# Experts' phase: the high and low parts of the 16 left-over rows as one operand

## The chip, the core and the metric

The kernel runs on one core of a Trainium2 chip. Time is device microseconds of one launch, lower is better. The engines of the core are named as the profile names them: PE is TensorE (with PEld for its weight loads), ACT is ScalarE, DVE is VectorE, POOL is GpSimd, and SP is the engine that here only issues DMAs. A name with a q behind it (PEldq, ACTq) is the sequencer of that engine.

## What is computed

Two layers over 16 sequences of 1024 tokens of width 256. The first layer normalizes, runs a recurrence and a mixture of experts, and multiplies the two; the second does the same with another recurrence and other experts. The change touches only the experts of the first layer:

```python
capacity = max(1, int(Sz * CAP_FACTOR / E) + 1)          # 1024 * 2 / 8 + 1 = 257
scores = softmax(einsum('bsd,ed->bse', x, router_w))
gate_vals, sel_idx = jax.lax.top_k(swapaxes(scores, 1, 2), capacity)
tokens = x[b_idx, sel_idx]                                # per expert 16 x 257 rows of 256
h = gelu(einsum('becd,edh->bech', tokens, w1) + b1, approximate=False)   # hidden width 1024
y = einsum('bech,ehd->becd', h, w2) + b2
out = zeros.at[b_idx, sel_idx].add(y * gate_vals[..., None])
```

Each of the 8 experts takes 257 rows of each of the 16 sequences: 4096 rows in 8 blocks of 512, and 16 rows left over, one of each sequence.

## The kernel before

The phases follow one another: routing, the first recurrence, the experts (`experts_phase`), layer 1. In `experts_phase` every engine has its own program, and semaphores alone order them. Each engine loops over experts 0 to 6 with one body and then runs expert 7 as straight code (`experts`, line 328; the loop itself, with its branch, has line 330).

**Precision.** Products run in float32r. To keep float32 accuracy each operand is split in a high part (a float32r copy, made by ACT) and a low part (the rest, made by DVE), and `product` (line 607) adds three matmuls for one: high x high, low x high, high x low. All of these matmuls have line 611.

**An expert on PE** (`one`, from line 640). Blocks q = 0 to 7 of 512 rows; for each of the 8 chunks m of the hidden width the up product (2 chunks of 128 of the input width, so 6 matmuls of 512 columns) is followed by one eighth of the down products of the block before (`down(e, q - 1, m)`, 12 matmuls of 256 columns). In the middle of a block (m = MID = 3) PE transposes the rows of the next block, or in the last block the 16 left-over rows (`turn_last`). For each m, ACT computes two gelus, one kept in float32 (`hf`) and one in float32r (`hTh`), and DVE subtracts them for the low part.

**The end of an expert.** Block 7's down products have no up products beside them: eight steps s = 0 to 7 (lines from 657). The left-over rows' up products go with the first four: 2 chunks of the hidden width in each step, 12 matmuls of 16 columns, 48 in all, into the bank `ps[2]`. After s = 3 PE transposes the first block of the next expert (`turn(e + 1, 0)`). Once all 48 are done ACT computes sixteen gelus of 128x16 (lines 477 and 478), with the bias b1 as the activation's own bias, and DVE makes the low part from them in one subtraction (line 562). ACT then makes the high part of the next expert's w1 (`split_up`, 434), DVE the low part (494), which lets SP issue the load of the w1 after that (342). The left-over down products (24 matmuls of 256 columns into `ps[4]`, with the 16 rows padded to 128 by zeros from two memsets at the phase's start, line 356) are PE's last work of the expert; DVE adds b2 (571) and multiplies by the gate (573), and POOL scatters the 16 rows (419). ACT's first step in the next turn of the loop is a gelu on one column (456), in front of which it loads its table.

**Waits that the change touches.** `up_ps` counts up products, and one more for all left-over ones; `hi_sb` counts gelus (8 of them for the left-over rows); `h_sb` low parts; `down_ps` halves of a block's down products and the left-over ones; `padded` the memsets. The banks `ps[0]` and `ps[1]` (tiles ps_heads in the profile, with ps[2] and ps[3]) hold transposes.

Of the kernel before, what the change touches and what calls it, by code (L numbers as in the profile page):

```python
# [5 lines left out]
ALU = mybir.AluOpType  # L6
# [251 lines left out]
def experts_phase(nc, ctx, ps, xn_d, acc_d, w1, b1, w2, b2, ident, idxT, gateT, idxL, gateL):  # L258

    with ExitStack() as mem:  # L260
        def sb(name, shape, dt=F32):
            return mem.enter_context(nc.sbuf_tensor(name, shape, dt))
# [23 lines left out]
        xTl = [sb(f"e_xTl{n}", [P, KD, B], F32R) for n in "hl"]  # L286
        hfl = sb("e_hfl", [P, HC, B])
        hTl = [sb(f"e_hTl{n}", [P, HC, P], F32R) for n in "hl"]
# [20 lines left out]
        down_ps = sem("e_down_ps")  # L309
        y_sum = sem("e_y_sum")  # L310
# [6 lines left out]
        HIGHS = QN * HC + HC  # L317
# [3 lines left out]
        MID = HC // 2 - 1  # L321
        W2_PARTS = 4
# [28 lines left out]
        def _(pool):  # L351
# [3 lines left out]
            for part in hTl:  # L355
                nc.gpsimd.memset(part[:].bitcast(F32), 0.0).then_inc(padded, 1)
# [74 lines left out]
        def _(act):  # L431
# [18 lines left out]
            def turn_last(e):  # L450
                act.wait_ge(turned, TURNS * e + QN + 1)
                nc.scalar.copy(xTl[0][:], ps[0][:, 0:KD * B].rearrange("p (k n) -> p k n", k=KD)).then_inc(xh_sb, 1)

            def one(e, last):
# [19 lines left out]
                act.wait_ge(up_ps, UPS * (e + 1))  # L474
                for m in range(HC):
                    z = ps[2][:, m * B:(m + 1) * B]
                    nc.scalar.activation(hfl[:, m, :], z, ACT.Gelu, bias=b1s[:, m:m + 1])
                    nc.scalar.activation(hTl[0][:, m, 0:B], z, ACT.Gelu, bias=b1s[:, m:m + 1]).then_inc(hi_sb, 1)
                if not last:

                    act.wait_ge(hi_sb, HIGHS * (e + 1) + 1)
                    split_up(e + 1)
                    turn(e + 1, 0)

            act.wait_ge(padded, 2)
# [5 lines left out]
        def _(dve):  # L491
# [24 lines left out]
            def turn_last(e):  # L516
                dve.wait_ge(xh_sb, TURNS * (e + 1))
                nc.vector.tensor_tensor(xTl[1][:], ps[0][:, 0:KD * B].rearrange("p (k n) -> p k n", k=KD),
                                        xTl[0][:].bitcast(F32), ALU.subtract).then_inc(xT_sb, 1)
# [23 lines left out]
            def one(e, last):  # L543

                dve.wait_ge(gts_set, 3 * e + 3)
                for q in range(QN):
                    for m in range(HC):
# [14 lines left out]
                nc.vector.tensor_tensor(hTl[1][:, :, 0:B], hfl[:], hTl[0][:, :, 0:B].bitcast(F32), ALU.subtract  # L562
# [8 lines left out]
                nc.vector.tensor_tensor(yl[:], ps[4][0:B, 0:D], b2s[0:B, :], ALU.add).then_inc(y_sum, 1)  # L571
# [13 lines left out]
        def _(pe):  # L585

            def turn(e, q):
                r = q % 2
                pe.wait_ge(x_in[r], 32 * QN * e + 64 * (q // 2) + 64)
                if not (isinstance(e, int) and e == 0 and q == 0):  # L590

                    pe.wait_ge(xT_sb, TURNS * e + q)
                for k in range(KD):
# [45 lines left out]

            def one(e, last):  # L640
# [13 lines left out]
                pe.wait_ge(xT_sb, TURNS * (e + 1))  # L654

                pe.wait_ge(hi_sb, HIGHS * e + HC * QN)
# [15 lines left out]
            pe.wait_ge(padded, 2)  # L672
# [1556 lines left out]
```

## Time and profile before

| | |
|---|---|
| Time, median of 3 runs | 4614.92 us (4613.5 to 4615.97) |
| Span of the profiled execution | 4612.0 us |
| Mean granted TensorE clock | 0.971 |
| Busy, share of the span | PE 91%, DVE 60%, ACT 43%, POOL 37% |
| Experts' phase, on PE | 1895 to 3510 us of the span |
| Slices of PE in that phase | 9 tenths or more in nearly each |

The page gives busy times of one execution. A busy PE is not a PE at its peak, since matmuls are pipelined and overlap: their duration is longer than the distance from one to the next. "issue" is idle time for which the profile shows no releaser. The granted clock is 1.00 for 2.4 GHz and 0.50 for 1.2 GHz.

### The profile page before, as it was taken

Reading aid. Unit: us, or ns where it says so; the run is one execution under the profiler, and the core shown is the slowest. Engines: PE = TensorE matmul, PEld = TensorE weight load, DVE = VectorE, ACT = ScalarE, POOL = GpSimd, SP = SyncE. Lnnn points to the kernel's source line nnn. Section 1 sums busy time; section 2 is a strip of 40 time slices with the busy share of each in tenths; the row PEclk is TensorE's granted clock in tenths of the full one; section 3 lists DMA queues with packets and bytes.
Section 4 is the critical chain, followed back from the end, with each engine's and each line's share of the span. In section 5 each row is a group of like instructions: output and inputs, shape, how many; then the busy total and the mean of one; then the engine's idle time right before and its main releaser. Section 6 shows DMA issues by size and latency. Waiting matters only on the chain. (4 is left out here: it accounts for less than half of the span.)

```text
span 4612.0 us, 79916 instructions
## 1 busy us (share of the span) xinstructions
PE 4189.6 (91%) x28828; PEld 3314.9 (72%) x28828; DVE 2751.5 (60%) x5151; ACT 1976.9 (43%) x3701; POOL 1694.4 (37%) x1338
## 2 busy tenths in 40 slices
PE   6759999999999999799999999999995989999985
PEld 6636555555555556698888989898995878777774
DVE  4447777777767777334343433434433688888886
ACT  2214444444444444444454444445442444444441
POOL 1123333333333333344444444444432233333333
PEclk9999999999999999899999999999997999999998
DMA  6611011011011010223223232323224334444433
GB/s 205 214 44 38 29 38 34 29 38 34 29 38 34 29 38 29 81 42 64 48 56 60 41 66 43 62 47 59 42 40 92 93 98 111 105 95 111 101 61 41
DMA packets 254043, 294.80 MB, mean 64 GB/s; under 512 B 21600, under 2 KB 226656, under 8 KB 251616
## 3 DMA queue, kind: packets, MB, share of 16 engines
q0 software_dynamic: 88064, 117.74, 15.2%
q1 hardware_dynamic: 140000, 138.26, 9.3%
q10 hardware_dynamic: 25600, 33.56, 2.2%
q8 instruction: 260, 4.26, 0.4%
q14 instruction: 119, 0.97, 0.1%
HBM read 155.15 MB, written 134.35 MB: 63 GB/s over the span
## 5 line engine op out<-in xcount | busy, mean ns | idle before, releaser
L523 DVE TENSOR_TENSOR e_hTl<-e_hf,e_hTh 128x512 fp32r<-128x512 f32 x512 | 355.0, 693 | 795.4 <-ACT e_hTh L465 795.4
L1018 POOL TENSOR_TENSOR a_mix<-a_tmp,a_h 128x512 f32<-128x512 f32 x320 | 393.9, 1251 | 808.4 <-DVE a_tmp L1105 651.9
L384 POOL DMA_INDIRECT acc_d<-e_y,e_sids x256 | 402.0, 1570 | 715.6 <-DVE e_y L539 670.8
L464 ACT ACTIVATE e_hf<-ps_heads,e_b 128x512 f32<-128x512 f32 x512 | 355.3, 694 | 697.8 <-PE ps_heads L611 690.6
L611 PE MATMUL ps<-e_w2h,e_hTh 128*128 128x256 f32 x2048 | 580.1, 283 | 0.0
L611 PE MATMUL ps<-e_w2h,e_hTl 128*128 128x256 f32 x2048 | 576.5, 281 | 0.0
L611 PE MATMUL ps<-e_w2l,e_hTh 128*128 128x256 f32 x2048 | 571.3, 279 | 0.0
L611 PE MATMUL ps_heads<-e_xTh,e_w1h 128*128 128x512 f32 x1024 | 419.4, 410 | 26.8 <-issue 22.8
L611 PE MATMUL ps_heads<-e_xTh,e_w1l 128*128 128x512 f32 x1024 | 407.6, 398 | 0.0
L611 PE MATMUL ps_heads<-e_xTl,e_w1h 128*128 128x512 f32 x1024 | 407.2, 398 | 0.4 <-issue 0.3
L611 PEld LDWEIGHTS ps<-e_w2h,e_hTh 128*128 128x128 f32 x2048 | 385.0, 188 | 19.8
L611 PEld LDWEIGHTS ps<-e_w2h,e_hTl 128*128 128x128 f32 x2048 | 385.0, 188 | 17.8
L611 PEld LDWEIGHTS ps<-e_w2l,e_hTh 128*128 128x128 f32 x2048 | 386.7, 189 | 0.0
L1408 PEld LDWEIGHTS ps_heads<-a_R,a_K 32*128 32x128 f32 x7168 | 227.0, 188 | 205.9 <-issue 204.2
L465 ACT ACTIVATE e_hTh<-ps_heads,e_b 128x512 fp32r<-128x512 f32 x512 | 351.3, 686 | 0.0
L1105 DVE SCALAR_TENSOR_TENSOR a_tmp<-ps,a_xb,a_delta 128x512 f32<-128x512 f32 x320 | 239.3, 750 | 174.9 <-PE ps L1317 160.8
L361 POOL DMA_INDIRECT e_x<-xn_d,e_gids x256 | 269.8, 1054 | 190.2 <-PE ps_heads L595 112.4
L1408 PE MATMUL ps_heads<-a_R,a_K 32*128 32x64 f32 x7168 | 256.8, 278 | 62.9 <-DVE a_A L1144 34.2
L1144 DVE COPY_PREDICATED a_A<-a_mask,ps_heads 128x1024 f32<-128x1024 uint32 x160 | 274.4, 1715 | 0.0
L1317 PE MATMUL ps<-a_x,a_xo 128*128 128x512 f32 x512 | 246.6, 604 | 0.7 <-ACT a_R L1231 0.7
L611 PEld LDWEIGHTS ps_heads<-e_xTh,e_w1h 128*128 128x128 f32 x1024 | 195.8, 191 | 66.9 <-issue 28.5
L611 PEld LDWEIGHTS ps_heads<-e_xTl,e_w1h 128*128 128x128 f32 x1024 | 195.3, 191 | 47.4
(294 smaller groups left out, 9458.6 us busy)
## 6 DMA issues: line engine op xcount, KB each, us to landing
r_x<-in_L_attn_hidden_states SPq DMA_DIRECT2D x32, 512.0 KB, 4.6
xn_d<-r_xn ACTq DMA_DIRECT2D x32, 512.0 KB, 3.1
xnT_d<-r_xT ACTq DMA_DIRECT2D x32, 512.0 KB, 3.6
acc_d<-a_zeros POOLq DMA_DIRECT2D x32, 512.0 KB, 3.0
s_d<-a_s SPq DMA_DIRECT2D x32, 512.0 KB, 2.8
e_w<-in_L_ffn_w SPq DMA_DIRECT2D x16, 1024.0 KB, 4.8
f_a<-acc_d SPq DMA_DIRECT2D x32, 512.0 KB, 3.8
f_x<-s_d SPq DMA_DIRECT2D x32, 512.0 KB, 5.2
```

Of the source, the lines that this page charges most:

```text
L361: pool.indirect_dma_start(xg[r][:, t, :], None, xn_d, bass.IndirectOffsetOnAxis(ap=gids[:, GT * q + t:GT * q + t + 1], axis=0)).then_inc(x ...
L384: pool.indirect_dma_start(acc_d, bass.IndirectOffsetOnAxis(ap=sids[:, GT * q + t:GT * q + t + 1], axis=0), ys[r][:, t, :], None, compute_o ...
L464: nc.scalar.activation(hf[m % 2][:], ps[2 + m % 2][:], ACT.Gelu, bias=b1s[:, m:m + 1])
L465: nc.scalar.activation(hT[q % 2][0][:, m, :], ps[2 + m % 2][:], ACT.Gelu, bias=b1s[:, m:m + 1]).then_inc(hi_sb, 1)
L523: nc.vector.tensor_tensor(hT[q % 2][1][:, m, :], hf[m % 2][:], hT[q % 2][0][:, m, :].bitcast(F32), ALU.subtract).then_inc(h_sb, 1)
L611: last = nc.tensor.matmul(out, lhsT, rhs, start=(first and n == 0), stop=(end and n == len(pairs) - 1))
L1018: nc.gpsimd.tensor_tensor(mix[n][:, m, :].rearrange("p (c t) -> p c t", c=GT), tmp[i % 2][:].rearrange("p (c t) -> p c t", c=GT), h[q % 2] ...
L1105: stt(out=tmp[i % 2][:], in0=bank(MIX[i])[:], scalar=xb[:, n, m:m + 1], in1=delta[r][:, m].rearrange("p c t -> p (c t)"), op0=ALU.add, op1 ...
L1144: nc.vector.copy_predicated(a4, m4.unsqueeze(1).to_broadcast([P, NH * GT, nb, half]), pairs_ps(half)).then_inc(A_sb, 1)
L1317: done = nc.tensor.matmul(to, lhsT, rhs, start=(k == 0), stop=(k == len(pairs) - 1))
L1408: done = nc.tensor.matmul(ps_heads[:, hd, c * P:c * P + P // 2].rearrange("p (n t) -> p n t", t=half), K2[r][rows, tok], R2[r][rows, tok]. ...
```

## The change

The high and low parts of the 16 left-over rows lie side by side in one tile and are one operand.

- Up: `xTl` is one tile with 32 columns (16 high, 16 low). Each chunk takes w1's high and low part times these 32 columns: 4 matmuls of 32 columns for 6 of 16, so 32 an expert for 48 (`up_last`). The fourth product, low x low, comes with it. They go to `ps[1]` and are placed in block 7 behind the up and down products of m = 4 to 7, two chunks each time.
- DVE adds the bias to the high columns and then the low columns, two adds of 128x128 into `zl`, and ACT computes two gelus of 128x128 on `zl` for the sixteen. `hi_sb` counts one for them.
- Down: `hTl` is one tile of 128 columns, the high part in columns 0 to 15, the low part in 32 to 47, the rest zeros from one memset. 16 matmuls for 24. The result stands on two groups of partitions; ACT copies the low one (`tl`, 16x256), DVE adds b2 to the high one and then `tl`.
- New waits: DVE waits for `up_ps` before the first add; ACT for `zl_o`, and at the end of the expert for `down_ps`; DVE for `tl_sb`; PE for `zl_o` before it transposes the next expert's first block, which overwrites `ps[1]`. PE no longer waits for the last gelus before the left-over up products.

```diff
@@ ACT, one(e, last)
-                act.wait_ge(up_ps, UPS * (e + 1))
-                for m in range(HC):
-                    z = ps[2][:, m * B:(m + 1) * B]
-                    nc.scalar.activation(hfl[:, m, :], z, ACT.Gelu, bias=b1s[:, m:m + 1])
-                    nc.scalar.activation(hTl[0][:, m, 0:B], z, ACT.Gelu, bias=b1s[:, m:m + 1]).then_inc(hi_sb, 1)
+                act.wait_ge(zl_o, 2 * e + 2)
+                nc.scalar.activation(hfl[:], zl[:], ACT.Gelu)
+                nc.scalar.activation(hTl[:, :, 0:B], zl[:], ACT.Gelu).then_inc(hi_sb, 1)
...
+                act.wait_ge(down_ps, DOWNS * (e + 1))
+                nc.scalar.copy(tl[:], ps[4][LOW_AT:LOW_AT + B, 0:D]).then_inc(tl_sb, 1)
@@ DVE, one(e, last)
+                dve.wait_ge(up_ps, UPS * (e + 1))
+                parts = ps[1][:, 0:HC * 2 * B].rearrange("p (m n) -> p m n", m=HC)
+                nc.vector.tensor_tensor(zl[:], parts[:, :, 0:B], b1s[:].unsqueeze(2).to_broadcast([P, HC, B]), ALU.add
+                                        ).then_inc(zl_o, 1)
+                dve.wait_ge(zl_o, 2 * e + 1)
+                nc.vector.tensor_tensor(zl[:], parts[:, :, B:2 * B], zl[:], ALU.add).then_inc(zl_o, 1)
                 result(e, QN - 2, 1)
...
-                nc.vector.tensor_tensor(yl[:], ps[4][0:B, 0:D], b2s[0:B, :], ALU.add).then_inc(y_sum, 1)
+                nc.vector.tensor_tensor(yl[:], ps[4][0:B, 0:D], b2s[0:B, :], ALU.add).then_inc(yl_o, 1)
+                dve.wait_ge(yl_o, e + 1)
+                dve.wait_ge(tl_sb, e + 1)
+                nc.vector.tensor_tensor(yl[:], yl[:], tl[:], ALU.add).then_inc(y_sum, 1)
@@ PE
+            def up_last(m, last):
+                for k in range(KD):
+                    for n, v in enumerate(w1p):
+                        ups = nc.tensor.matmul(ps[1][:, m * 2 * B:(m + 1) * 2 * B], v[:, k, m * P:(m + 1) * P], xTl[:, k, :],
+                                               start=(k == 0 and n == 0), stop=(k == KD - 1 and n == 1))
+                if last:
+                    ups.then_inc(up_ps, 1)
...
+                        if q == QN - 1 and m > MID:
+                            if m == MID + 1:
+                                pe.wait_ge(xT_sb, TURNS * (e + 1))
+                            for n in (2 * (m - MID) - 2, 2 * (m - MID) - 1):
+                                up_last(n, n == HC - 1)
                 for s in range(HC):
-                    if s <= MID:
-                        for m in (2 * s, 2 * s + 1):
-                            ups = product(ps[2][:, m * B:(m + 1) * B], [([w[:, k, m * P:(m + 1) * P] for w in w1p],
-                                                                         [v[:, k, :] for v in xTl]) for k in range(KD)])
-                        if s == MID:
-                            ups.then_inc(up_ps, 1)
                     down(e, QN - 1, s)
...
-                product(ps[4][:, 0:D], [([v[:, m, :] for v in hTl], [w[:, m, :] for w in w2p]) for m in range(HC)]
-                        ).then_inc(down_ps, 1)
+                for m in range(HC):
+                    for n, v in enumerate(w2p):
+                        done = nc.tensor.matmul(ps[4][:, 0:D], hTl[:, m, :], v[:, m, :], start=(m == 0 and n == 0),
+                                                stop=(m == HC - 1 and n == 1))
+                done.then_inc(down_ps, 1)
```

## Rows read from the trace of the kernel before

**Rows 1.** Groups by line, PE, 1895 to 3515 us: busy, mean ns, idle before

```profile
L611 PE MATMUL ps_heads<-e_xTh,e_w1h 128*128 128x512 f32 x1024 | 419.4, 410 | 26.8 <-issue 22.8 <-DVE e_xTl L512 2.6 <-ACT e_hTh L465 0.5
...
L595 PE MATMUL ps_heads<-ident,e_x 128*128 128x128 f32 x512 | 67.2, 275 | 14.9 <-DMA e_x<-xn_d,e_gids 14.9
```

**Rows 2.** Timeline of PE (start, duration), left-over up products of expert 0

```profile
2077.92 0.17 PE L611 MATMUL ps_heads<-e_xTlh,e_w1h 128*128 128x16 f32 x1
...
2079.38 0.28 PE L611 MATMUL ps<-e_w2h,e_hTl 128*128 128x256 f32 x1
```

**Rows 3.** Timeline of PE: left-over down products, then the next expert

```profile
2095.52 0.28 PE L611 MATMUL ps<-e_w2h,e_hTlh 128*128 128x256 f32 x1
...
2098.24 0.28 PE L611 MATMUL ps<-e_w2l,e_hTlh 128*128 128x256 f32 x1
2101.88 0.79 PE L611 MATMUL ps_heads<-e_xTh,e_w1h 128*128 128x512 f32 x1 [3.36 <-issue]
```

**Rows 4.** Loop lines (330 experts, 895 recurrence, 1615 layer 1): ns min/median/max, first and last start

```profile
L330 ACTq COMPARE_BRANCH  x7: 40/45/50, 2090.7 to 3306.3; - x7
...
L330 PEldq COMPARE_BRANCH  x7: 82/5407/6047, 2096.3 to 3311.9; - x7
...
L895 PEldq COMPARE_BRANCH  x6: 83/4320/4557, 692.4 to 1683.0; - x6
...
L1615 PEldq COMPARE_BRANCH  x2: 83/1826/3570, 4042.8 to 4294.1; - x2
```

**Rows 5.** SP's timeline; DMA queues and issues (size, us to landing) around the branch

```profile
2095.05 0.33 SPq L342 DMA_DIRECT2D e_w<-in_L_ffn_w  x1
...
q1 hardware_dynamic: 288, 1.05, 52.1%
...
q8 instruction: 1, 0.02, 1.0%
...
e_w<-in_L_ffn_w SPq DMA_DIRECT2D x1, 1024.0 KB, 4.6
```

**Rows 6.** Timelines of DVE and ACT at the end of expert 0

```profile
2078.00 0.69 DVE L523 TENSOR_TENSOR e_hTl<-e_hf,e_hTh 128x512 fp32r<-128x512 f32 x1 [2.12 <-ACT e_hTh L465]
...
2090.42 0.29 DVE L562 TENSOR_TENSOR e_hTll<-e_hfl,e_hTlh 128x128 fp32r<-128x128 f32 x1 [10.48 <-ACT e_hTlh L478]
2092.53 2.29 DVE L494 TENSOR_TENSOR e_w1l<-e_w,e_w1h 128x2048 fp32r<-128x2048 f32 x1 [1.82 <-ACT e_b L435]
...
2099.79 0.27 DVE L506 COPY e_b<-e_b2i 128x256 f32<-128x256 f32 x1
...
2093.49 1.28 ACT L456 ACT_TABLE_LOAD   x1
```

**Rows 7.** Timeline of POOL, last expert's left-over scatter

```profile
3513.04 1.30 POOL L419 DMA_INDIRECT acc_d<-e_yl,e_sidl  x1 [0.30 <-issue]
```

**Rows 8.** Timeline of POOL at the start of the experts' phase

```profile
1886.41 0.95 POOL L356 MEMSET e_hTll<- 128x1024 f32 x1
```

**Rows 9.** Groups by line, ACT in the recurrence

```profile
L1240 ACT ACTIVATE a_A<-ident,a_own 128x128 f32<-128x128 f32 x512 | 153.2, 387 | 1.0
```

**Rows 10.** Stretches: length, busy (count) of PE, PEld, DVE, ACT, POOL; granted clock; DMA

```profile
2101.88:2105.10 3.22, 3.22 (x8) 2.54 (x9) 0.00 (x0) 0.26 (x1) 2.61 (x3) 0.50 0.59 65
...
sum 99.87, PE 98.45 PEld 72.70 DVE 51.73 ACT 75.87 POOL 68.15; mean PE 16.41 PEld 12.12 DVE 8.62 ACT 12.64 POOL 11.36
...
3313.94:3328.64 14.70, 14.47 (x64) 10.62 (x63) 10.08 (x20) 12.64 (x22) 10.22 (x10) 1.00 0.41 57
```

**Rows 11.** Two gaps in layer 1 (PE's timeline) and the stretch behind each

```profile
3669.96 1.09 PE L2051 MATMUL ps_heads<-ident,f_xn 128*128 128x128 f32 x8 [2.81 <-ACT f_xn L1958]
...
3787.25 1.17 PE L2051 MATMUL ps_heads<-ident,f_xn 128*128 128x128 f32 x7 [2.15 <-ACT f_xn L1958]
...
3670.00:3673.40 3.40, 3.40 (x30) 3.40 (x31) 3.27 (x6) 2.15 (x5) 2.27 (x2) 1.00 0.31 104
3788.00:3791.20 3.20, 3.20 (x17) 3.20 (x16) 3.10 (x7) 1.18 (x2) 1.33 (x1) 0.50 0.31 20
```

More of the change, by code:

```diff
@@ L285, in experts_phase @@
         xl = sb("e_xl", [B, D])
-        xTl = [sb(f"e_xTl{n}", [P, KD, B], F32R) for n in "hl"]
+        xTl = sb("e_xTl", [P, KD, 2 * B], F32R)
+        zl = sb("e_zl", [P, HC, B])
         hfl = sb("e_hfl", [P, HC, B])
-        hTl = [sb(f"e_hTl{n}", [P, HC, P], F32R) for n in "hl"]
+        hTl = sb("e_hTl", [P, HC, P], F32R)
+        tl = sb("e_tl", [B, D])
         yl = sb("e_yl", [B, D])
@@ L309, in experts_phase @@
         down_ps = sem("e_down_ps")
+        zl_o = sem("e_zl_o")
+        tl_sb = sem("e_tl_sb")
+        yl_o = sem("e_yl_o")
         y_sum = sem("e_y_sum")
@@ L316, in experts_phase @@
         UPS = QN * HC + 1
-        HIGHS = QN * HC + HC
+        HIGHS = QN * HC + 1
         LOWS = QN * HC + 1
@@ L321, in experts_phase @@
         MID = HC // 2 - 1
+        LOW_AT = 2 * B
         W2_PARTS = 4
@@ L354, in _ @@
             pool.sem_inc(w2_split, W2_PARTS)
-            for part in hTl:
-                nc.gpsimd.memset(part[:].bitcast(F32), 0.0).then_inc(padded, 1)
+            nc.gpsimd.memset(hTl[:].bitcast(F32), 0.0).then_inc(padded, 1)
             def gather(q):
@@ L451, in turn_last @@
                 act.wait_ge(turned, TURNS * e + QN + 1)
-                nc.scalar.copy(xTl[0][:], ps[0][:, 0:KD * B].rearrange("p (k n) -> p k n", k=KD)).then_inc(xh_sb, 1)
+                nc.scalar.copy(xTl[:, :, 0:B], ps[0][:, 0:KD * B].rearrange("p (k n) -> p k n", k=KD)).then_inc(xh_sb, 1)
             def one(e, last):
@@ L483, in one @@
                     turn(e + 1, 0)
-            act.wait_ge(padded, 2)
+                act.wait_ge(down_ps, DOWNS * (e + 1))
+                nc.scalar.copy(tl[:], ps[4][LOW_AT:LOW_AT + B, 0:D]).then_inc(tl_sb, 1)
+            act.wait_ge(padded, 1)
             split_up(0)
@@ L517, in turn_last @@
                 dve.wait_ge(xh_sb, TURNS * (e + 1))
-                nc.vector.tensor_tensor(xTl[1][:], ps[0][:, 0:KD * B].rearrange("p (k n) -> p k n", k=KD),
-                                        xTl[0][:].bitcast(F32), ALU.subtract).then_inc(xT_sb, 1)
+                nc.vector.tensor_tensor(xTl[:, :, B:2 * B], ps[0][:, 0:KD * B].rearrange("p (k n) -> p k n", k=KD),
+                                        xTl[:, :, 0:B].bitcast(F32), ALU.subtract).then_inc(xT_sb, 1)
             def low(e, q, m):
@@ L559, in one @@
                             split_down(e, W2_AT[m])
+                dve.wait_ge(up_ps, UPS * (e + 1))
[4 more added lines that the diff above has]
+                nc.vector.tensor_tensor(zl[:], parts[:, :, B:2 * B], zl[:], ALU.add).then_inc(zl_o, 1)
                 result(e, QN - 2, 1)
                 dve.wait_ge(hi_sb, HIGHS * (e + 1) + 1)
-                nc.vector.tensor_tensor(hTl[1][:, :, 0:B], hfl[:], hTl[0][:, :, 0:B].bitcast(F32), ALU.subtract
+                nc.vector.tensor_tensor(hTl[:, :, LOW_AT:LOW_AT + B], hfl[:], hTl[:, :, 0:B].bitcast(F32), ALU.subtract
                                         ).then_inc(h_sb, 1)
@@ L592, in turn @@
                     pe.wait_ge(xT_sb, TURNS * e + q)
+                    if isinstance(q, int) and q == 0:
+                        pe.wait_ge(zl_o, 2 * e)
                 for k in range(KD):
@@ L668, in one @@
                 pe.wait_ge(y_sum, YS * e + 2 * (QN - 1) + 1)
-                product(ps[4][:, 0:D], [([v[:, m, :] for v in hTl], [w[:, m, :] for w in w2p]) for m in range(HC)]
-                        ).then_inc(down_ps, 1)
-            pe.wait_ge(padded, 2)
+                for m in range(HC):
[3 more added lines that the diff above has]
+                done.then_inc(down_ps, 1)
+            pe.wait_ge(padded, 1)
             turn(0, 0)
```

2 lines of the change are left out of this document (removed).

## The prediction

> **What bounds the kernel now.** The page's busy shares and slices come first (they are in the table above): TensorE (PE) is busy nearly all the time in the experts' phase, to which the changed lines belong. Next I read the groups by line for that phase [rows 1], to see what idle time PE has left in its 1615 us: 22.8 us "issue" in front of the up products, and 14.9 us on the first gather. So PE's own work is the path, and a PE instruction taken away is a gain unless another engine is late at the next meeting point.
>
> A duration is no price here, because products overlap; the price is the pitch, start to start. The twelve 16-column products that begin at 2077.92 hold the 256-column ones up until 2079.38, where the second of them starts [rows 2]: 1.46 - 0.12 for the first = 1.34 us for 12, so **0.112 us** each. The 24 left-over down products start between 2095.52 and 2098.24 [rows 3]: 2.72 us for 23 steps, **0.118 us** each.
>
> Then the end of an expert. After the last product ends (2098.24 + 0.28 = 2098.52, called T below) PE stands still for 3.36 us [rows 3]; six such gaps make up the 22.8 us, 3.8 us in the mean. They aren't a wait for data: DVE's last copies there end at 2100.06 [rows 6] and are nothing that PE asks for. The rows of the loops' own lines say what they are [rows 4]: PE's branch back to the top lasts 5.4 us in the median and up to 6.05, the same branch on ACT 45 ns. PE's body isn't at hand and is fetched. (The minimum of 82 ns is the last turn, which falls through.) In the recurrence's loop the branch takes PE 4.3 us, in layer 1's the one taken 3.57. What differs stands in the DMA rows [rows 5]: in the 6 us of the experts' branch queue 1 moves 1.05 MB and fills half of all 16 engines, the load of the next w1 that SP issued at 2095.05, and the one instruction packet of queue 8 goes with it. So I read 5.4 - 3.57 = 1.8 us of the median branch as the fetch standing behind the w1 load.
>
> **Part by part.**
> (1) Up projection: 32 products of 32 columns for 48 of 16. None of 32 is in the trace. The nearest rows are 0.112 at 16 columns and, above, 0.118 at 256 [rows 2, 3]; I take 0.112, since 240 more columns add only 0.006. Gain 16 x 0.112 = 1.79 us an expert, **14.3 us** (48 x 0.112 - 32 x 0.118 = 1.6 each, 12.8, at the upper end). Their new place behind ups 4 to 7 costs nothing: DVE ends the last block's low part at 2078.69 [rows 6], the last downs begin at 2077.92 [rows 2], and their second step, the first that needs it, comes 12 x 0.118 = 1.42 us later even if nothing lies between.
> One sentence that the sum doesn't need: the Trainium skill, "TensorE: Matmul & The Clock Gate", section "Back-to-back issue gap", gives some 81 ns a product for a stream of loads and products of 128 columns, by which an estimate of (1) would be 16 x 8 x 0.081 = 10.4 us; the row of 16 columns says 0.112 here, and the row decides.
> (2) Down projection: 16 products for 24, 8 x 0.118 = 0.95 us an expert. In the last expert it is hidden: POOL's last scatter, at 3513.04, waited for nothing but its own issue [rows 7]. 7 x 0.95 = **6.6 us**.
> (3) One memset for two in front of the first gather: POOL's second takes 0.95 us [rows 8], the gathers follow it, and PE waits for them [rows 1]. **0.9 us**.
> (4) Two gelus of 128 columns for sixteen of 16, and early. Now DVE gets the sixteen's results at 2090.42, starts w1's low half 2.1 us later at 2092.53 (ACT makes the high half between), and SP issues the next w1 load when that is done, 2095.05 [rows 5, 6]. In the new order this chain hangs on the early up products. Let u be the start of the last up step, a step of ups (6 products, 1.40) and one of downs (1.42) before 2077.92, so 2075.10. Left-over ups done: u + 1.4 + 1.4 + 8 x 0.112 + 0.3 = u + 4.0. Two adds on DVE, 0.29 each as the 128x128 one of [rows 6]: u + 4.7. Two gelus, 0.39 each [rows 9]: u + 5.4. Then 2.1 and 2.29 as before: u + 9.8, SP's load at u + 10.1. T is at u + 3.7 + 8 x 1.42 + 0.8 (eight transposes) + 16 x 0.118 + 0.2 = u + 18.0, and PE's branch is issued 2.2 us ahead of T (the first starts at 2096.3 [rows 4]), at u + 15.8. The load takes 4.6 us [rows 5] and ends at u + 14.7, **1.1 us before the branch** and no longer in it. The branch then lasts as in layer 1, 3.57, or as in the recurrence, 4.3; I take the first. Of the branch 2.2 us lie ahead of T, and some 0.3 follow until the first product starts, so a gap is the branch less 1.9 us (5.4 less 1.9 is 3.5, near the mean of 3.8; the longest, 6.05, gives 4.1): 1.7 to 1.8 us for 3.8. 2.0 x 6 = **12 us** (7 at 4.3; 0 if the fetch isn't shortened). POOL's small scatters lie in the branch before and after.
> (5) The clock. After the gap the granted clock is 0.50, the lower level of 1.2 GHz, for some 3 us [rows 10]. From an expert's first up product to its first down product the six turns take 99.87 us, 16.6 each; the last expert, which PE enters without a gap, takes 14.70 at 2.4 GHz: 99.9 - 88.2 = 11.7 us lost to the slow clock. Whether a gap of 1.8 us is still followed by it is open: one of 2.15 us is, one of 2.81 us isn't [rows 11]. I take half, **6 us**, with 0 and 12 as ends.
> (6) Added: a copy of 16x256 by ACT behind the last product, a second add on DVE, and PE's wait on zl_o ahead of the next expert's transposes. No row shows this copy; activations of 128x128 take 0.39 us [rows 9], and I take 0.4 of 0.2 to 0.6. What stands behind it in ACT's queue is the branch (0.05), the table load (1.28 [rows 6]) and the table's gelu (0.2 to 0.4): ACT is ready at T + 2.1. Its first real gelu is due when the first up is done, T + 1.8 + 1.6 = T + 3.4. DVE is done at T + 1.5 now, with a second add and its wait at T + 2.1; its first low part is due at T + 4.7. PE's wait on zl_o is met at u + 4.7, and the transposes come at u + 9.4. DVE has the result of block 6 (1.3 us) behind the new adds, and nobody asks for it before the left-over downs. **0**, covered by PE's branch and first up; without that cover it costs what exceeds T + 3.4.
>
> Sum: 14.3 + 6.6 + 0.9 + 12 + 6 = 39.8 us. The profiled execution has a span of 4612.0 us, which gives 4572.2; the median of the runs stands 2.9 us above that span, so **4575 us**.
>
> **Rivals.** (A) The forecast; its own range goes from 14.3 + 6.6 + 0.9 + 7 + 0 = 29 us to 22 + 12 + 12 = 46: 4569 to 4586.
> (B) The branch isn't shortened, since what it waits for isn't the load, or something else takes the load's place. For it: the branch is long in every loop. Against it: the 1.8 us to layer 1's. Only the counts remain, 22 us: **4593 us**.
> The Trainium skill has a rule on this, "DMA: Bandwidth & Descriptors", section "Queues, rings and completion order": a DMA engine changes between queues only after a whole packet, typically 9 to 17 descriptors. The 288 pieces of the load's window over 16 engines are 18 each, about one such packet, which would hold the fetch to its end (A); were the pieces passed singly, the fetch would lose little to the load, and B would hold.
> (C) The shorter last product only uncovers the branch: if PE's sequencer reached the branch at a fixed time and not a fixed number of products before T, 0.95 us would be given back six times. 5.7 us less, **4581 us**, inside A's range.
> (D) The change doesn't do what it says, because a product of 32 columns costs half as much again as one of 16 (0.168): (1) is nothing, the rest stays, **4589 us**. The 0.118 at 256 columns speaks against it.
> (E) Slower: ACT, which now waits for the last product before it turns back, fetches its own body in the open. With a fetch of s it is ready at T + 2.1 + s, and what exceeds T + 3.4 is paid six times. From s = 8 us on it takes the whole gain (6 x 6.7 = 40); at 9.5 it gives **4624 us**. ACT's branch row, never over 50 ns [rows 4], speaks against it.
>
> **How the numbers follow.** A 0.62, C 0.08, B 0.20, D 0.03, E 0.02, and 0.05 for something between B and no gain. 4575 is A's value. The range runs from A's best case to B's value, with 2 us at either side for the scatter of executions: 4567 to 4595, which leaves out some 0.1 to 0.15. About 0.2%, 9.2 us, is what a measurement of this kernel can tell from no change; faster is then below 4605.7, as A to D all are: 0.95; same 0.03; slower 0.02.
>
> **What would show it.** In the profile after: 256 products of 32 columns, pitch 0.112 us; the w1 load issued some 8 us before T; the branch row of the experts' loop near 3.6 us, and "issue" before the up products near 11 us and not 22.8; first up to first down at 14.7 us in some turns. It would be wrong with gaps of 3.8 us though the load is gone from them (B), with ACT or DVE named as what PE waits for at the start of an expert (E), or with the load still in the branch, if DVE comes late to w1's low half.

## The result and the profile after

The changed kernel takes **4578.48 us** in the median of 4 runs (4577.81 to 4583.38), against 4615.44 us for the kernel before on the same chip (4613.5 to 4621.8). The ratio is 0.9922, with a 95% interval of 0.9908 to 0.9936. The profiled execution has a span of 4577.2 us for 4612.0, 34.8 us less, at a mean granted clock of 0.972 for 0.971.

Groups by line, PE, the experts' phase of the changed kernel (busy, mean ns, idle before). They answer [rows 1], with the left-over products as new groups:

```profile
L627 PE MATMUL ps_heads<-e_xTh,e_w1h 128*128 128x512 f32 x1024 | 418.0, 408 | 16.5 <-issue 12.4 <-DVE e_xTl L517 2.6 <-ACT e_hTh L470 0.3
L627 PE MATMUL ps_heads<-e_xTl,e_w1h 128*128 128x512 f32 x1024 | 404.4, 395 | 3.8 <-issue 3.8
L659 PE MATMUL ps_heads<-e_xTl,e_w1l 128*128 128x32 f32 x128 | 29.8, 263 | 0.0
L659 PE MATMUL ps_heads<-e_xTl,e_w1h 128*128 128x32 f32 x128 | 27.2, 242 | 0.0
```

The "issue" time in front of an expert's first product fell from 22.8 us to 12.4. What the sum did not have is the second line: 3.8 us of "issue" in front of another product, the ninth of an expert, where before there was 0.4.

PE's timeline (start, duration): seven of a step's eight left-over up products (first and last shown), the left-over down products, and the start of expert 1. It answers [rows 2, 3]:

```profile
2079.11 0.26 PE L659 MATMUL ps_heads<-e_xTl,e_w1l 128*128 128x32 f32 x1
...
2079.78 0.26 PE L659 MATMUL ps_heads<-e_xTl,e_w1l 128*128 128x32 f32 x1
...
2092.20 0.28 PE L691 MATMUL ps<-e_w2h,e_hTl 128*128 128x256 f32 x1
...
2093.98 0.27 PE L691 MATMUL ps<-e_w2l,e_hTl 128*128 128x256 f32 x1
2095.95 0.49 PE L627 MATMUL ps_heads<-e_xTh,e_w1h 128*128 128x512 f32 x1 [1.69 <-issue]
...
2097.68 0.40 PE L627 MATMUL ps_heads<-e_xTh,e_w1l 128*128 128x512 f32 x1
2098.71 0.39 PE L627 MATMUL ps_heads<-e_xTl,e_w1h 128*128 128x512 f32 x1 [0.64 <-issue]
```

Six steps in 0.67 us are 0.112 us a product of 32 columns, as for 16 before. The sixteen down products take 15 steps in 1.78 us, 0.119 each. The end of the last one, T, is 2094.25 here. The gap behind it is 1.69 us for 3.36, and after eight products of the new expert PE stands still a second time.

The loop's own line (336 here; ns min/median/max, first and last start). It answers [rows 4]:

```profile
L336 PEldq COMPARE_BRANCH  x7: 83/3838/4122, 2092.1 to 3276.9; - x7
L336 ACTq COMPARE_BRANCH  x7: 40/45/50, 2094.4 to 3279.2; - x7
```

SP's timeline, and behind it the packets by queue (packets, MB, share of 16 engines) from the start of PE's branch to where PE goes on, 2092.1 to 2095.6. They answer [rows 5]:

```profile
2085.91 0.33 SPq L348 DMA_DIRECT2D e_w<-in_L_ffn_w  x1
```

```profile
q0 software_dynamic: 145, 0.13, 30.7%
q8 instruction: 1, 0.02, 1.7%
```

The w1 load is issued 6.2 us ahead of the branch and 8.3 ahead of T; queue 1, which had 288 packets there before, has none. The branch takes 3.84 us in the median for 5.41. These medians are of seven, with the last turn, which falls through, among them; the mean of the six branches taken is 3.85 us for 5.64. The instruction packet, queue 8, starts 1.1 to 1.5 us after the branch does, for 2.8 to 3.7 before.

Timelines of ACT and then of DVE around T. They answer [rows 6]:

```profile
2080.73 0.31 ACT L480 ACTIVATE e_hfl<-e_zl 128x128 f32<-128x128 f32 x1 [1.60 <-DVE e_zl L570]
...
2094.29 0.36 ACT L488 COPY e_tl<-ps 16x256 f32<-16x256 f32 x1 [6.48 <-PE ps L691]
2094.68 1.28 ACT L461 ACT_TABLE_LOAD   x1
2095.98 0.20 ACT L461 ACTIVATE e_table<-ident 128x1 f32<-128x1 f32 x1
2097.64 0.69 ACT L469 ACTIVATE e_hf<-ps_heads,e_b 128x512 f32<-128x512 f32 x1 [1.47 <-PE ps_heads L627]
```

```profile
2083.39 2.29 DVE L499 TENSOR_TENSOR e_w1l<-e_w,e_w1h 128x2048 fp32r<-128x2048 f32 x1 [1.24 <-ACT e_b L440]
...
2096.21 0.27 DVE L511 COPY e_b<-e_b2i 128x256 f32<-128x256 f32 x1
```

w1's low half starts 10.9 us ahead of T (6.0 before), and ACT, which has the new copy behind the last product, is ready at T + 1.9 and then waits another 1.47 us for PE.

Stretches of PE from an expert's first up product to its first down product, experts 0 to 7 (length, busy and count, granted clock, share and GB/s of the DMA engines; the ends of most are rounded by up to 0.06 us). They answer [rows 10]:

```profile
1898.22:1914.90 16.68, 16.49 (x63) 0.88 0.34 97
2095.95:2111.50 15.55, 14.73 (x63) 1.00 0.36 63
2293.15:2308.95 15.80, 14.71 (x62) 1.00 0.36 64
2490.41:2506.50 16.09, 14.72 (x62) 1.00 0.38 70
2687.97:2703.90 15.93, 14.71 (x62) 1.00 0.36 67
2885.66:2902.00 16.34, 16.12 (x62) 0.90 0.36 66
3083.45:3099.70 16.25, 16.06 (x62) 0.90 0.36 68
3278.94:3293.60 14.66, 14.43 (x64) 1.00 0.30 52
```

Four of the six turns now stay at 2.4 GHz, and still none of them is near the 14.7 of the last expert: about 1.1 us of each is idle. By the products' own starts the six add up to 96.1 us and the last expert's is 14.72.

**Where the 34.8 us are.** Worked out from the starts in PE's timeline, expert by expert:

| | before | after | less |
|---|---|---|---|
| first down product to T, seven experts | 182.14 each | 179.39 each | 19.3 |
| the same in the last expert, as far as POOL's last scatter shows it | | | 1.8 |
| six gaps at the branch | 22.8 | 12.4 | 10.4 |
| first up to first down, six turns after a branch | 99.9 | 96.1 | 3.8 |
| PE's wait for the first gather | 14.95 | 14.67 | 0.3 |
| unchanged code: recurrence ends earlier | | | 1.4 |
| unchanged code: from POOL's first memset of layer 1 to the end | 1089.1 | 1091.0 | -1.9 |

These are 35.1 us, 0.3 more than the span's 34.8. Two stretches that the table leaves out are 0.1 us longer each: expert 0's own first part (16.64 for 16.50) and the time from the last scatter's start to the memset of layer 1 (9.98 for 9.86).

### The profile page after: what moved, and what is told of

It is laid out like the page before. It is cut to its first block and busy times, and to the rows that moved or that the text cites. A ratio compares the mean times of both kernels' runs of the same rounds, so it can differ in the third digit from the quotient of the medians.

```text
span 4577.2 us, 79367 instructions
## 1 busy us (share of the span) xinstructions
PE 4157.1 (91%) x28636; PEld 3286.4 (72%) x28636; DVE 2764.4 (60%) x5175; ACT 1962.4 (43%) x3597; POOL 1702.2 (37%) x1337
## 5 line engine op out<-in xcount | busy, mean ns | idle before, releaser
L389 POOL DMA_INDIRECT acc_d<-e_y,e_sids x256 | 411.6, 1608 | 674.8 <-DVE e_y L544 630.0
L627 PE MATMUL ps_heads<-e_xTh,e_w1h 128*128 128x512 f32 x1024 | 418.0, 408 | 16.5 <-issue 12.4
```

The costliest lines, as they stand in the source:

```text
L389: pool.indirect_dma_start(acc_d, bass.IndirectOffsetOnAxis(ap=sids[:, GT * q + t:GT * q + t + 1], axis=0), ys[r][:, t, :], None, compute_o ...
L627: last = nc.tensor.matmul(out, lhsT, rhs, start=(first and n == 0), stop=(end and n == len(pairs) - 1))
```

## The experiments

**The theory.** The sum is made of the product counts, of the w1 load that leaves the branch, and of the clock. **The rival**: the shorter gap has to do with where the code lies and how long it is, or with the gelus, and the load is a bystander. Three kernels move the load alone or the placement alone.

**1. The changed kernel with the load put back.**

```diff
                 sp.wait_ge(w1_split, e + 1)
+                sp.wait_ge(late, e + 1)
...
                 scatter(e, QN - 1, 0)
+                pool.sem_inc(late, 1)
                 scatter(e, QN - 1, 1)
```

POOL also raises the new semaphore at the start of the phase, by 2 here and by 1 in experiment 2, so that the first loads do not wait for it.

> The changed kernel, with one thing undone: SyncE may issue the next expert's w1 load only when GpSimd has finished the first half of the last block's scatters, which puts it back to some half a microsecond before TensorE's branch, as in the kernel before. Product counts, gelus and adds stay as changed. Theory (the fetch of the branch's target stands behind the load): TensorE's branch row goes back from 3.8 to over 5 us, the gaps in front of an expert's first up product from 2.1 to about 3.5 to 4 us each, the clock falls after most of them; 6 x 1.7 = 10 us and some of the clock's, so 10 to 14 us over the changed kernel, about 4590, a ratio of about 0.9945 to the kernel before. Rival (the shorter gap comes from the body's shorter code and its place, not from the load): branch and gaps stay as in the changed kernel, 4578, 0.992. A second rival: w1 arrives late for the split; then the idle time stands at the next w1 split, not at the branch.

Measured: 4589.7 us (4588.43 to 4592.24), ratio 0.9945 (0.9931 to 0.9958). Loop line of that kernel:

```profile
L337 PEldq COMPARE_BRANCH  x7: 83/4902/5257, 2092.0 to 3286.9; - x7
```

Packets by queue in its first branch, from 2092.06 to 2094.3 and then to 2094.6:

```profile
q0 software_dynamic: 230, 0.22, 61.4%
q1 hardware_dynamic: 197, 0.39, 48.0%
...
q1 hardware_dynamic: 198, 0.40, 43.1%
q8 instruction: 1, 0.02, 2.3%
```

The branch is 1.06 us longer, the gaps are 18.9 us for 12.4 in sum, and the parts behind them 99.7 for 96.1: 10.0 us, of the 11.2 measured. The instruction packet (queue 8) starts within those last 0.3 us, when nearly all of the load is through: three of its 128 packets of 8 KB still start behind it. In the next four branches the load's last packet ends 0.8 to 1.3 us before the instruction packet starts, while POOL's scatter packets (queue 0) run until 0.1 us after its start. So the fetch stands here behind what the load and the scatters together have in the engines, and not behind the load alone; which packet holds it these runs don't separate. The load had in fact gone out 3.6 us before the branch, not half a microsecond, and was slower (5.4 us to landing), sharing the engines with POOL's scatters. So the size was hit and the dose was not what I had meant.

**2. The kernel before with the load moved behind the branch**, by a semaphore that ACT gives after the second block of gelus of the next expert; nothing of the change is in it.

```diff
                 sp.wait_ge(w1_split, e + 1)
+                sp.wait_ge(late, e + 1)
...
+                        if q == 0 and m == 1:
+                            act.sem_inc(late, 1)
```

> The kernel before, with one thing done: the next expert's w1 load is held by SyncE until ScalarE has made the second gelu of the next expert, so that it lies some 4 us behind the branch and not in it. The w1 is not needed until the end of that expert. Theory: the branch row goes from 5.4 us to about 3.8, the six gaps from 22.8 us in sum to about 12, the clock falls less often; 8 to 14 us less than the kernel before, 4601 to 4607, ratio about 0.9975. Rival (the code's length and place set the branch): nothing changes, ratio 1.000.

Measured: 4601.51 us (4599.23 to 4605.39), ratio 0.9969 (0.9956 to 0.9981), 12.5 us less than before.

```profile
L331 PEldq COMPARE_BRANCH  x7: 83/3702/3892, 2098.1 to 3301.1; - x7
```

The gaps are 11.1 us in sum for 22.8. That is the whole of term (4), had with one semaphore and without the change, so the load's place in time is the cause of the long branch. The load goes out 7.8 to 9.7 us after the branch starts, and no data packet at all starts between a branch and its instruction packet, which follows 0.9 to 1.6 us after the branch's start.

**3. The changed kernel with its up products back in the last block's downs.**

```diff
-                        if q == QN - 1 and m > MID:
-                            ...
-                            for n in (2 * (m - MID) - 2, 2 * (m - MID) - 1):
-                                up_last(n, n == HC - 1)
                 for s in range(HC):
+                    if s <= MID:
+                        for n in (2 * s, 2 * s + 1):
+                            up_last(n, n == HC - 1)
                     down(e, QN - 1, s)
```

With it the products go back to the bank `ps[2]`, DVE's result of block 6 stands ahead of its two adds again, and PE waits for the last gelus again instead of `zl_o`.

> The changed kernel, with the placement undone alone: the left-over up products (still 32, of 32 columns) stand again among the first four steps of the last block's downs, in the bank they had, the rest as changed. That makes the chain zl, gelus, w1 split and w1 load later by some 5 us. Theory: the counts' gain (some 21 us) stays, the load is issued about 3 us before T and lies in the branch, the gaps are about 3.8 us again: 4592 to 4596, ratio about 0.9955. Rival (placement is irrelevant, since the two gelus for sixteen already free ScalarE): about 4578 to 4580, 0.9923.

Measured: 4589.88 us (4586.82 to 4592.79), ratio 0.9945 (0.9931 to 0.9958).

```profile
L336 PEldq COMPARE_BRANCH  x7: 82/4947/5137, 2096.3 to 3290.6; - x7
```

SP's timeline there:

```profile
2094.42 0.33 SPq L348 DMA_DIRECT2D e_w<-in_L_ffn_w  x1
```

First down to T stays 179.38 us, the counts' gain in full; the gaps are 19.0 us again. The load goes out 1.9 us ahead of the branch instead of 1.3 as before, 0.6 earlier, and the mean of the six branches is 4.99 us for 5.64, 0.65 less: 3.8 us of the gaps in sum, and the time is 2 us under my range. Against the changed kernel the placement is worth 11.4 us; the rest of the change, without it, 24.2.

The five kernels in order of the load's issue against the branch:

| kernel | load issued | branch, median of the row | mean of the six taken | six gaps |
|---|---|---|---|---|
| before | 1.3 us ahead | 5.41 | 5.64 | 22.8 |
| 3 | 1.9 us ahead | 4.95 | 4.99 | 19.0 |
| 1 | 3.6 us ahead | 4.90 | 4.92 | 18.9 |
| after | 6.2 us ahead | 3.84 | 3.85 | 12.4 |
| 2 | 7.8 to 9.7 us behind | 3.70 | 3.69 | 11.1 |

**4. What the branch costs in all.** PE's loop in the changed kernel with two experts in a turn, then with three, and the last two experts behind it, so that two branches or one are left of six:

```diff
+                with eng.Fori(0, NE // 2 - 1) as h:
+                    one(2 * h, False)
+                    one(2 * h + 1, False)
+                one(NE - 2, False)
+                one(NE - 1, True)
```

> The changed kernel, with TensorE's loop over the experts written with two experts in one turn and the last two outside: of six branches back only two are taken. Nothing that is computed or its order changes. Theory (gap, the second stall of about 0.9 us behind it, and the slow clock are all what the branch costs): the four turns without a branch have no gap, no second stall and full clock: 4 x 2.1 + about 3 + about 1 = 12 us less than the changed kernel, 4566, ratio about 0.9895; ScalarE's table load ends at T + 1.9 and its first gelu is asked for by the third up block only at T + 2.8, so it stays covered. Rival 1: without the gap ScalarE or VectorE is late, and a wait on them takes its place: less than half of the gain, 4572 or more. Rival 2: the longer code stalls TensorE's fetch elsewhere: new issue time in the middle of an expert, no gain.

> The changed kernel, with TensorE's loop over the experts written with three experts in one turn and the last two outside: of six branches back only one is taken (with two in a turn, two were taken; that gave 12.1 us less from the first to the last expert's start, and 8.2 us less in the median, as the last phase, whose code is unchanged, took 4.5 us longer in the profile). Theory: each branch less gives 3 us (gap 2.1 less than nothing, second stall, clock): 3 us less than that kernel, 4567, ratio 0.9895 to 0.9900. Rival: the gain of pairs was near its end and what follows (ScalarE's and VectorE's late start, 0.4 us a turn) takes the rest: 4570.

Measured: two in a turn 4570.32 us (4568.14 to 4574.04), ratio 0.9903 (0.9888 to 0.9918); three 4561.16 us (4557.02 to 4564.72), ratio 0.9884 (0.9869 to 0.9899), **17.3 us less than the changed kernel**. From the first expert's first up product to the last expert's, 1380.72 us became 1368.61 with two in a turn and 1365.31 with three, 12.1 and another 3.3 less, as expected. The medians don't follow so neatly (8.2 and another 9.2 less), since the last phase, whose code is the same, took from T of the last expert 1109.7 us with two in a turn and 1103.2 with three, for 1105.0 in the changed kernel. Why it differs stays open. One part of the expectation failed: ScalarE does not stay covered, PE waits 0.45 us for it in each turn without a branch.

Stretches of the kernel with three in a turn, first up to first down, without and with a branch ahead:

```profile
2093.59:2108.69 15.10, 14.53 (x64) 1.00 0.34 53
2484.46:2500.73 16.27, 16.10 (x62) 0.90 0.36 65
```

PE's timeline in the first of them, its one wait of more than 0.1 us:

```profile
2097.01 0.50 PE L636 MATMUL ps_heads<-e_xTh,e_w1h 128*128 128x512 f32 x1 [0.45 <-ACT e_hTh L479]
```

**5. The kernel before with three experts in a turn**, the same edit with nothing of the change. It asks what the change is worth where the branch is nearly gone.

> The kernel before, with TensorE's expert loop written with three experts in a turn and the last two outside, as in the changed kernel of that form (4561 us); nothing of the change is in it. One branch is left. Theory (the gain is the counts, and apart from them only what the branch costs): without five of the six branches the kernel before loses 5 x 3.8 = 19 us of gaps and some 5 x 1.9 = 9 us of slow clock, 28 us: 4586; against it the changed kernel's form of 4561 is 25 us less, of which 21 are counts, and the rest the one branch left. Rival (the change has another source of gain that isn't the branch, or the up products or gelus in their old place cost time of their own): the difference between the two forms stays near 37 us, this kernel at 4598. Rival the other way (the counts are worth less than the pitch says): this kernel under 4578.

Measured: 4583.87 us (4581.74 to 4585.3), ratio 0.9936 (0.9922 to 0.9949). The changed kernel in this form is 22.7 us faster by the medians, against 37.0 us with all branches; the counts of the ledger above are 21.1 of the 22.7. In the profiles the one branch left gives another 2.3 us (gap 2.06 us for 3.43, the stretch behind it 16.27 for 17.18) and a wait on ACT in five turns takes 2.2 back, so some 1.5 us of the medians' difference stay open. Stretches without and with a branch ahead:

```profile
2098.23:2112.87 14.64, 14.46 (x65) 1.00 0.47 79
2495.05:2512.23 17.18, 17.00 (x63) 0.84 0.34 64
```

Here the turn without a branch is 14.64 us and not 15.10: the 0.45 us wait on ACT above is what the change itself adds, hidden by the branch in the changed kernel and bare once the branch is gone.

**6. ACT's loop in the same form**, to take out the table load behind the new copy:

```diff
             turn(0, 0)
+            tripled.append(act)
             experts(act, one)
```

> The changed kernel, with three experts in a turn on TensorE and on ScalarE. On ScalarE the reload of its table (1.28 us, once for each pass of its loop's body, behind the copy of tl) is then left out in the turns that don't branch. Theory (the 0.4 us by which an expert's first part is longer than 14.7 in the turns without a branch is ScalarE's late start behind that reload): 15.1 goes to 14.7 in five turns, 2 us less than the form with TensorE alone, 4559, ratio 0.988. Rival (VectorE, with its second add and the gates' copies, is as late): 15.1 stays, 4561.

Measured: 4557.1 us (4554.6 to 4558.89), ratio 0.9880 (0.9865 to 0.9896). ACT's group for the table loads:

```profile
L470 ACT ACT_TABLE_LOAD x2 | 2.6, 1283 | 2.3 <-issue 2.3
```

ACT's timeline at the end of expert 0, and PE's stretch behind it:

```profile
2095.38 0.36 ACT L497 COPY e_tl<-ps 16x256 f32<-16x256 f32 x1 [6.48 <-PE ps L701]
2095.65 0.20 ACT L470 ACTIVATE e_table<-ident 128x1 f32<-128x1 f32 x1
```

```profile
2095.18:2109.84 14.66, 14.51 (x64) 1.00 0.30 46
```

Two table loads are left of seven, and 15.10 is 14.66. This is the fastest kernel of the study, 21.4 us under the changed one by the medians; from the first expert's start to the last's it takes 1363.43 us, 1.9 less than the form with PE alone, as expected. The intervals of the two overlap, and the other 2 us between the medians may be the last phase again (1096.8 us in this profile).

**7. The second stall.** In the changed kernel it comes after the eighth product of an expert. If the first instruction packet ends there, it must move with the code. The same line, with 24 and with 12:

```diff
             turn(0, 0)
+            for _ in range(24):
+                pe.sem_inc(spare, 1)
             experts(pe, one)
```

> The changed kernel, with 24 increments of a spare semaphore that nobody waits for in front of TensorE's loop over the experts. They only move the loop's body further along in TensorE's code, in which instructions come in packets of 16 KB; the stall of about 0.9 us that TensorE shows after the eighth product of an expert, in the turns that come in at full clock, stands with a second instruction packet that follows the branch's. Theory (that stall is the place where the loop's first packet ends, so it moves with the code): with the body at the start of a packet the stall after the eighth product is gone or lies far behind it where it is covered; 3.8 us less than the changed kernel in sum, 4574 to 4576, ratio about 0.9914. Rival (the stall comes from TensorE's waits or from data, whatever the code's place): unchanged, 0.9922, with 3 to 4 us issue in front of the products of e_xTl as before.

> As the kernel with 24 increments, with 12: the body moves by half of that. Theory: the second stall moves by a few products, to earlier in the first up block (after some 2 of them), and is no shorter; the branch's own row is unchanged at 3.8 us. Rival: the stall stays after the eighth product.

> The changed kernel with 12 spare increments in front of TensorE's expert loop again, now timed (the single look gave 4598.9 us: 13.5 us of idle time in front of the second product of an expert, and the first part of an expert at 19.2 us in six turns). If the code's place is what costs it, every execution shows it: 4594 to 4600, ratio near 0.9965, 20 us over the changed kernel, with 24 increments not. If the look was a stray one: 4578.

Measured: with 24, 4578.26 us (4573.67 to 4581.76), ratio 0.9919 (0.9906 to 0.9933), no difference from the changed kernel; with 12, 4598.9 us in one run and then, in the median of five, 4594.15 us (4592.36 to 4602.65), ratio 0.9965 (0.9951 to 0.9979): **12 instructions that do nothing, run once, cost 15.7 us** by the medians, and 18.1 us from the first to the last expert's start in the profiles. PE's timeline behind the branch and the stretch there, with 12 (timed kernel):

```profile
2095.42 0.54 PE L627 MATMUL ps_heads<-e_xTh,e_w1h 128*128 128x512 f32 x1 [2.13 <-issue]
2095.76 0.63 PE L627 MATMUL ps_heads<-e_xTh,e_w1l 128*128 128x512 f32 x1
2098.14 0.59 PE L627 MATMUL ps_heads<-e_xTl,e_w1h 128*128 128x512 f32 x1 [1.75 <-issue]
```

```profile
2095.42:2114.26 18.84, 16.91 (x62) 0.82 0.37 74
```

With 24, PE's group that had the 3.8 us, and two of the stretches:

```profile
L627 PE MATMUL ps_heads<-e_xTl,e_w1h 128*128 128x512 f32 x1024 | 406.5, 397 | 0.0
```

```profile
2099.05:2115.33 16.28, 16.09 (x63) 0.90 0.36 66
...
2691.78:2706.53 14.75, 14.59 (x63) 1.00 0.35 63
```

The stall moved from behind the eighth product (0.64 to 1.20 us in four turns) to behind the second (1.75 to 2.82 us in six), 13.4 us of idle time in sum for 3.8, and with 24 it is gone. So it belongs to the place of the code, as the theory says. Queue 8 in PE's first microsecond of expert 1, in the changed kernel (2095.95 to 2096.9) and with 12 (2095.42 to 2096.2), has the second instruction packet:

```profile
q8 instruction: 1, 0.02, 6.1%
q8 instruction: 1, 0.02, 7.4%
```

In the changed kernel's six turns it starts 0.3 to 0.5 us after an expert's first product, and so it does with 12, and the product behind the stall starts 2.3 to 3.1 us after the packet does. What differs is the work that PE has in hand until then: eight products, some 2.1 us at full clock, or two. In the two slow turns of the changed kernel eight products last 3.5 us and cover the wait whole. So a full clock up to the ninth product gains next to nothing there: that product starts 2.8 to 3.3 us after the first in the four fast turns, and 3.5 to 3.6 in the two slow ones.

The gain of 3.8 us that I expected from the stall's going did not come: without the stall the clock fell in five of the six turns (16.0 to 16.3 us each) for two of six with it, and the six parts are 95.95 us in sum for 96.1. That the missing stall makes the clock fall is not shown: in experiment 8, where PE's products and their order are those of the changed kernel and the stall is in its old place, the clock fell in five of six turns too, with 97.3 us for the six parts. These counts are of one profiled execution each. I had said that the stall would be no shorter with 12; that it would be so much longer I had not foreseen.

**8. The second memset put back**, into a tile that nobody reads, ahead of POOL's first gather.

```diff
             nc.gpsimd.memset(hTl[:].bitcast(F32), 0.0).then_inc(padded, 1)
+            nc.gpsimd.memset(hTl2[:], 0.0).then_inc(padded, 1)
...
-            act.wait_ge(padded, 1)
+            act.wait_ge(padded, 2)
...
-            pe.wait_ge(padded, 1)
+            pe.wait_ge(padded, 2)
```

> The changed kernel with a second memset of the same size (into a tile that nothing reads) in front of GpSimd's first gathers, as before the change. Theory (GpSimd's order of instructions alone sets the gathers): TensorE's first transposes of the experts' phase start 0.9 us later after the end of the phase ahead. Rival (the gathers wait behind the w1 and w2 loads in the DMA engines, so that their issue hardly matters): some 0.3 us or less. The whole time can't tell this apart; the rows between GpSimd's memset and TensorE's first transpose do.

Measured: 4584.33 us in the one run. POOL's timeline, and then PE's group for the transposes:

```profile
1889.77 0.95 POOL L363 MEMSET e_hTl<- 128x1024 f32 x1
```

```profile
L613 PE MATMUL ps_heads<-ident,e_x 128*128 128x128 f32 x512 | 67.2, 275 | 14.8 <-DMA e_x<-xn_d,e_gids 14.8
```

PE waits 14.84 us for 14.67 in the changed kernel: 0.2 us for 0.9. Among all kernels here the wait lies between 14.6 and 15.5 us with one memset and between 14.8 and 15.9 with two. What of the term exists is within that scatter. The 6 us that the whole run is longer lie elsewhere: PE's first transpose of this phase comes 5.1 us later, of which the end of the recurrence, unchanged code, has 4.9.

## Why the prediction was right

**Forecast A** held: 4575 was said, 4578.48 measured, inside A's own range of 4569 to 4586. By its steps:

(1) and (2), **the counts**: 20.9 us said, 21.1 found. The 32-column product has the pitch of the 16-column one, 0.112 us, so (D) falls. An expert's part from the first down product to T is 2.75 us shorter, where 1.79 + 0.95 = 2.74 was said. The last expert gives about 1.8 us of its 2.7, since POOL's scatters end it, as said. Experiment 3 keeps the part at 179.38 us with the placement undone.

(3), **the memset**: 0.9 us said, 0.3 at most found. The failed step is that PE waits for POOL's order of instructions. It waits for the gathers' data, and their issue 0.9 us earlier brought that data 0.2 us earlier (experiment 8), no more than the scatter between kernels.

(4), **the load out of the branch**: 12 us said, 10.4 found in the gaps. The chain was right in each link: w1's low half was said at u + 7.5, or T - 10.5, and came at T - 10.9; the load at T - 7.9, and came at T - 8.3. Experiment 2 shows the cause with the load alone. What was mis-sized is the floor: I took 3.57 us, the one taken branch of layer 1, which lies between 3.3 and 3.9 us in the profiles of this study; here it is 3.85 in the mean, and 3.69 even with no load anywhere near. The 5.4 us that the prediction reads for the branch before is the median with the last turn's fall-through, and the six branches taken have a mean of 5.64; the sum goes by the gaps and doesn't use it. Rival (B) is out, and (C) is within the term and can't be told from that floor.

The Trainium skill, "DMA: Bandwidth & Descriptors", section "Queues, rings and completion order", was weighed in the prediction for such a hold-up by whole packets of descriptors. The trace agrees in what comes out of it (before the change the instruction packet starts 2.8 to 3.7 us after the branch, within 0.3 us of the end of the load's last packet), but doesn't show the rule itself at work. The prediction's 18 pieces an engine were misread: of the 288 packets 128 are the load's, of 8 KB, 8 an engine, and the rest are smaller ones.

(5), **the clock**: 6 us said, 8.4 found, and then 4.5 of it lost. The six parts exceeded the 14.72 us of an undisturbed turn by 11.6 us in sum before, 0.4 of it the second stall and the rest slow clock. After, two turns are slow and exceed it by 3.2 us; the other four are at full clock and exceed it by 4.5, of which 3.8 are the second stall's idle time. The net is 3.8 us in this execution; by the parts of experiment 8, where five turns were slow, it would be 2.6. That the term came out at roughly half of what was said is luck more than insight, since the stall wasn't in it. Half was taken for want of knowledge, and the runs bear the doubt out: gaps of 1.69 to 2.25 us were not followed by the slow clock in four turns, gaps of 2.03 and 2.35 were. No length of the gap tells them apart here, and with the stall gone (24 increments) the clock falls in five turns with gaps no longer than these (1.95 to 2.14 us), and in experiment 8 in five with 1.96 to 2.25.

What the prediction lacked is the **second instruction packet**: behind a branch PE works with the packet of its target until the next one, which starts 0.3 to 0.5 us after the first product, has come, and how far it gets until then depends on where the loop's top lies (experiment 7). The Trainium skill, "Runtime: NRT & Kernel Launch", section "Instruction fetch mechanics", has both halves: a taken branch breaks the prefetch, which goes on in sequence, and crossing into the next block is mostly hidden. The trace agrees with the first (3.3 us and more for each taken branch of PE in the experts' loop) and not with the second where the crossing comes right behind a branch: 0.64 to 1.20 us bare in four turns of the changed kernel, 1.75 to 2.82 with 12 increments.

(6), **the added work**: nothing said, nothing found in the changed kernel; ACT is ready at T + 1.9 (T + 2.1 said) and waits 1.47 us. The condition named with it, "without that cover it costs", came true in experiment 4: with the branch gone ACT is 0.45 us late in each turn, and experiment 6 takes that away. (E) is out, at 45 ns for ACT's branch.

By terms: 21.1 + 0.3 + 10.4 + 3.8 = 35.6 us for the 39.8 said. The unchanged code before and behind took 0.5 us of that back (1.4 less, 1.9 more), which no term can hold.

## What to carry to other kernels

Rows of the loops' own lines, read beside the DMA rows of the same microseconds, tell of a cost that the groups by engine show only as "issue": a large load issued shortly ahead of a long engine program's branch back delays the fetch of that program, and moving the load alone was worth 12.5 us here. Before reworking the arithmetic at a loop's end, try the cheap edits first: the load's issue time, several bodies in one turn (17 us here, 21 with ACT), or nothing at all but a few instructions ahead of the loop, which moved this kernel by 16 us the wrong way. And count what a branch hides: an engine that is 0.45 us late shows only once the branch is gone.

## What the runs showed of the hardware

- PE's taken branch over this body takes 3.3 to 3.9 us where no data packet starts between it and its instruction packet (experiment 2), 3.5 to 4.1 with POOL's scatters there, and 5.2 to 6.05 us with a 1 MB load issued 1.3 us ahead. The instruction packet starts 0.9 to 1.6, 1.1 to 1.5 and 2.8 to 3.7 us into it, and the branch ends 2.3 to 2.9 us after that in all three. ACT's and DVE's branches take 45 and 56 ns in the same loop.
- The fetch of the next packet behind a branch can leave PE idle again: 0.64 to 1.20 us after 8 products at full clock, nothing after 8 products at the slow one in the changed kernel, 1.75 to 2.82 us after 2, none with the code shifted further.
- One branch of PE costs 3.5 us in the changed kernel: 15.4 us from the first to the last expert for five avoided, 3.1 each, and the 0.45 us of ACT that each uncovers. The gap that one sees at it is 2.1 us of that.
- A gap of 1.7 to 2.4 us at the branch was sometimes followed by 1.2 GHz for 3 us or more and sometimes not, with no difference in its length.
- The same unchanged code of the last phase took 1097 to 1110 us from the last expert's end, from kernel to kernel: more than several of the terms argued over here.
